# Latent attention rebuilt with keys on the partitions: the sums of probabilities added up in SBUF by GpSimd, one product with ones per batch

## The reference

```python
def layernorm(x, g, b):
    mu = jnp.mean(x, axis=-1, keepdims=True)
    var = jnp.mean(jnp.square(x - mu), axis=-1, keepdims=True)
    return (x - mu) * jax.lax.rsqrt(var + LN_EPS) * g + b

def rmsnorm(x, gamma):
    n = jnp.linalg.norm(x, axis=-1, keepdims=True) * x.shape[-1] ** (-0.5)
    return x / jnp.maximum(n, RMS_EPS) * gamma
xn = layernorm(x, ln_x_g, ln_x_b)            # x here: the context
ln = layernorm(latents, ln_l_g, ln_l_b)      # latents: the tokens
q = ln @ W_q
kv = jnp.concatenate([xn @ W_kv, ln @ W_kv], axis=1)
...
qn = rmsnorm(q, q_gamma) * SCALE
kn = rmsnorm(k, k_gamma)
sim = jnp.einsum('bhid,bhjd->bhij', qn, kn)
sim = jnp.where(full_mask[:, None, None, :], sim, neg)
attn = jax.nn.softmax(sim.astype(jnp.float32), axis=-1).astype(sim.dtype)
out = jnp.einsum('bhij,bhjd->bhid', attn, v)
...
return out @ W_out + b_out
```

## Time and profile before

| | us |
|---|---|
| median of 3 runs (6344.28 to 6349.45) | 6347.48 |
| the profiled execution | 6344.81 |
| its span, first to last instruction | 6343.0 |
| TensorE busy over the span (mean granted clock 0.840) | 4691.1 |
| latent sublayer, first transfer issued to last instruction | 3683.22 to 4145.88 |

### The profile page before, as it was taken

How to read it: one execution, slowest core, us unless ns; L and a number is a source line. 1 busy time by engine, 2 the same in 40 slices (tenths; PEclk the granted TensorE clock), 3 DMA queues, 4 the chain that set the end, 5 groups by cost and what they waited for, 6 DMA issues and landing times. The chain is left out here.

```text
span 6343.0 us, 136570 instructions
## 1 busy us (share of the span) xinstructions
PE 4691.1 (74%) x46654; PEld 2666.1 (42%) x46654; DVE 3568.5 (56%) x6692; ACT 2632.4 (42%) x5390; POOL 1186.4 (19%) x2741
## 2 busy tenths in 40 slices
PE   1101766785757989595888557789999999999997
PEld 0101222332332222243333245566676667666674
DVE  7897433544436666434333533266776677676775
ACT  0101632452635756251111111156665666656664
POOL 0000100010100101110000000034444344443442
PEclk6555878896968989696999755589999999999998
DMA  1000000000000000000000000010000000000000
GB/s 28 0 0 2 1 10 14 1 1 3 1 31 1 1 1 1 11 1 20 24 22 23 8 4 0 0 41 6 9 20 9 20 6 24 5 24 5 13 16 10
DMA packets 46808, 66.67 MB, mean 11 GB/s; under 512 B 8628, under 2 KB 40480, under 8 KB 44977
## 3 DMA queue, kind: packets, MB, share of 16 engines
q1 hardware_dynamic: 45564, 58.16, 3.1%
q0 software_dynamic: 784, 1.80, 0.1%
HBM read 53.22 MB, written 1.05 MB: 9 GB/s over the span
## 5 line engine op out<-in xcount | busy, mean ns | idle before, releaser
L647 DVE TENSOR_REDUCE minus_max<-banks 128x1 f32<-128x512 f32 (+4 forms) x1152 | 608.4, 570 | 308.7 <-PE banks L541 300.5
L611 ACT ACTIVATE probs<-banks 128x512 f32<-128x512 f32 (+4 forms) x1152 | 580.7, 554 | 349.3 <-PE banks L579 344.2
L2345 POOL TENSOR_TENSOR loc_cos_part<-loc_cos_part,loc_sin_part 128x512 f32<-128x512 f32 x388 | 494.1, 1274 | 741.5 <-DVE loc_sin_part L2774 741.3
L592 PE MATMUL banks<-probs,pair_rows 128*32 128x512 f32 (+3 forms) x2304 | 564.8, 573 | 0.2 <-ACT probs L611 0.2
L2418 PE MATMUL banks<-loc_w_qkv,loc_shifted 128*128 (+1 forms) x1552 | 416.1, 414 | 81.8 <-issue 66.5
L1301 DVE TENSOR_TENSOR product<-gated,banks 128x512 f32<-128x512 f32 x168 | 115.6, 688 | 489.9 <-ACT gated L1283 489.9
L1842 PE MATMUL banks<-identity,srt_c 128*128 128x128 f32 x64 | 13.6, 370 | 492.8 <-DVE srt_c L1970 492.8
L212 POOL TENSOR_SCALAR fin_shifted<-fin_moments 128x4 f32<-128x4 f32 x48 | 14.4, 299 | 1901.2 <-DVE fin_moments L298 1901.2
L1283 ACT ACTIVATE gated<-banks 128x512 f32<-128x512 f32 x168 | 100.3, 597 | 612.6 <-PE banks L1239 612.6
L2418 PEld LDWEIGHTS banks<-loc_w_qkv,loc_shifted 128*128 128x128 f32 x1552 | 295.8, 201 | 128.9 <-issue 68.8
L2771 DVE TENSOR_TENSOR loc_cos_part<-banks,loc_table 128x512 f32<-128x512 f32 x388 | 264.5, 682 | 73.8 <-ACT loc_square L2639 73.6
(11 more groups left out here) (471 smaller groups left out, 10180.4 us busy)
## 6 DMA issues: line engine op xcount, KB each, us to landing
expert_w<-in_L_ffn_pairs_dram SPq DMA_DIRECT2D x84, 192.0 KB, 2.4
loc_w_qkv<-in_L_ffn_Wqkv_dram SPq DMA_DIRECT2D x7, 1536.0 KB
q_stack<-max_rows SPq DMA_DIRECT2D x384, 3.0 KB
loc_v_edge<-loc_v SPq DMA_DIRECT2D x192, 32.0 KB, 1.8
fixed_w<-in_L_ffn_experts_dram SPq DMA_DIRECT2D x8, 514.5 KB, 4.1
loc_pack<-in_L_ffn_pack_dram SPq DMA_DIRECT2D x6, 537.5 KB, 4.3
loc_w_o<-in_L_ffn_Wo_dram SPq DMA_DIRECT2D x6, 512.0 KB, 4.1
loc_scales<-in_L_ffn_scales_dram SPq DMA_DIRECT2D x7, 256.0 KB, 8.0
```

Of the source, the lines that this page charges most:

```text
L592: ins = nc.tensor.matmul(o_bank[at:at + COLS, q0:S], pair_rows[u][:, k, e, :], probs[(a * C + k) % RING][e][:, q0:S], start=(k == 0), stop ...
L611: nc.scalar.activation(probs[(a * C + k) % RING][e][0:kn, q0:S], t_bank[e][0:kn, q0:S], ACT.Exp, scale=scale).then_inc(s["exp_done"], 1)
L647: nc.vector.tensor_reduce(minus_max[:, u, e, qs[0]:qs[0] + len(qs)], view, AX.X, ALU.max, negate=True).then_inc(s["max_done"], 1)
L2345: nc.gpsimd.tensor_tensor(cos_part[:, tiles, :], cos_part[:, tiles, :], sin_part[:, tiles, :], ALU.add).then_inc(s["summed"], 1)
```

## The change

The sublayer becomes three steps that share tiles: `latent_projections` (q, k, v for all four batches), `latent_heads` (attention for all), and `finish(..., "turned", ...)`, where the heads already stand with features on the partitions, so that the transposes and their copies fall away. The block that only loaded weights is gone; SyncE issues the transfers in the first block, beside the first statistics.

In `latent_projections` the batches are unrolled. TensorE's order is turn(0), and for each batch products(b), turn(b+1), means(b). The products now put features on the partitions (512 columns at a time), the squares are ScalarE's, their mean over a head is a product with a matrix of 1/64 (`means`), and the inverse root is ScalarE's Ln and then Exp with scale -0.5, three and two instructions per batch. VectorE's order per batch is copy_k(b), statistics(b+2), normalise(b+1), scale(b).

In `latent_heads` the scores are computed twice: `direct`, with queries on the partitions, only for the maxima (as before, but both heads at a time), and `turned`, with keys on the partitions, for exp. The maximum is split in three bf16 parts by GpSimd, turned by TensorE (`turn_maxima`), and added to the turned scores by a product with ones. So the probabilities come out with keys on the partitions, and neither transposes nor copies stand ahead of the product with v. The sum over keys: GpSimd adds the six key tiles of a head together in SBUF (`add`), and one product with ones per head and batch (`sums`) adds over the partitions. Head e uses rows 64e to 64e+63 of TensorE in `direct` and `turned`, and its columns in `values` and `sums`. RING = 4 buffers of probabilities per head, two pairs of `totals`.

```diff
@@ finish @@
+    if source == "turned":
+        pe.wait_ge(s["y_copied"], b + 1)
+        for t in range(QT):
+            ins = nc.tensor.matmul(g.bank[2 + u][:, t * P:(t + 1) * P],
+                                   y_now[:, u, t * P:(t + 1) * P], w_out[:, :],
+                                   start=True, stop=False)
+            ins = nc.tensor.matmul(g.bank[2 + u][:, t * P:(t + 1) * P],
+                                   g.ones[0:1, 0:P], bias_row[0:1, :],
+                                   start=False, stop=True)
...
@@ latent_projections, tensor @@
+def products(b):
+    u = b % 2
...
+    nc.tensor.matmul(g.bank[2][:, :], w_q[:, :], zT[u][:, 0:S], start=True, stop=True)
+    nc.tensor.matmul(g.bank[3][:, :], w_kv[:, 0:D], zT[u][:, 0:S], start=True,
+                     stop=True).then_inc(s["products_ready"], 1)
+    for t in range(QT, TILES):
+        nc.tensor.matmul(g.bank[4][:, (t - 2) * P:(t - 1) * P], zT[u][:, t * P:(t + 1) * P],
+                         w_kv[:, D:2 * D], start=True, stop=True)
+    nc.tensor.matmul(g.bank[4][:, 0:2 * P], w_kv[:, 0:D], zT[u][:, S:ALL], start=True,
+                     stop=True).then_inc(s["products_ready"], 1)
...
+def means(b):
+    pe.wait_ge(s["squared"], b * 3 + 3)
+    pe.wait_ge(s["q_copied"], b + 1)
+    if b:
+        pe.wait_ge(s["log_done"], b * 3)
+    lhs = mean_of[:, :, :].rearrange("p h d -> p (h d)")
+    for bank, c0, c1 in ((g.bank[2][:, 0:2 * P], 2 * S, S + ALL), (g.bank[6][:, :], 0, S),
+                         (g.bank[7][:, :], S, 2 * S)):
+        nc.tensor.matmul(bank, lhs, square[:, c0:c1], start=True, stop=True).then_inc(s["mean_ready"], 1)
...
+turn(0)
+for b in range(B):
+    products(b)
+    if b + 1 < B:
+        turn(b + 1)
+    if b == 0:
+        pe.wait_ge(s["setup"], 4)
+    means(b)
@@ latent_projections, scalar and vector @@
+def inverses(b):
+    for i, (bank, c0, c1) in enumerate(((g.bank[2][:, 0:2 * P], 2 * S, S + ALL), (g.bank[6][:, :], 0, S),
+                                        (g.bank[7][:, :], S, 2 * S))):
+        act.wait_ge(s["mean_ready"], b * 3 + i + 1)
+        nc.scalar.activation(log[:, c0:c1], bank, ACT.Ln).then_inc(s["log_done"], 1)
+    if b:
+        act.wait_ge(s["scaled"], b * 2)
+    act.wait_ge(s["log_done"], b * 3 + 3)
+    for c0, c1 in ((0, S), (S, S + ALL)):
+        nc.scalar.activation(inverse[:, c0:c1], log[:, c0:c1], ACT.Exp, scale=-0.5).then_inc(s["inverse_done"], 1)
+copy_zT(0)
+for b in range(B):
+    squares(b)
+    if b + 1 < B:
+        copy_zT(b + 1)
+    inverses(b)
...
+for b in range(B):
+    copy_k(b)
+    if b + 2 < B:
+        statistics(b + 2)
+    if b + 1 < B:
+        normalise(b + 1)
+    scale(b)
@@ latent_heads @@
+def direct(b, q):
+    n = b * QT + q
+    if n:
+        pe.wait_ge(s["max_done"], n * 2)
+    here = slice(q * P, (q + 1) * P)
+    for e in range(HEADS):
+        nc.tensor.matmul(g.bank[2 + e][:, 0:CTX], ones_bf[half(e), :], bias_rows[half(e), b, :],
+                         start=True, stop=False, skip_group_check=True)
+    for e in range(HEADS):
+        nc.tensor.matmul(g.bank[2 + e][:, 0:CTX], qT[b][half(e), here], kT[b][half(e), S:S + CTX],
+                         start=False, stop=True, skip_group_check=True)
+    for e in range(HEADS):
+        nc.tensor.matmul(g.bank[e][:, :], qT[b][half(e), here], kT[b][half(e), 0:S],
+                         start=True, stop=True).then_inc(s["direct_ready"], 1)
+def turn_maxima(b):
+    pe.wait_ge(s["third_done"], b + 1)
+    if b:
+        pe.wait_ge(s["rows_copied"], b)
+    for q in range(QT):
+        ins = nc.tensor.matmul(x_bank[:, q * P:(q + 1) * P],
+                               max_parts[:, q, :, :].rearrange("p e i -> p (e i)"), g.ident_bf[:, :],
+                               start=True, stop=True)
+    ins.then_inc(s["max_turned"], 1)
+def turned(b, k):
+    m = b * TILES + k
+    if k == 0:
+        pe.wait_ge(s["rows_copied"], b + 1)
+    if m:
+        pe.wait_ge(s["exp_done"], m * 2)
+    for e in range(HEADS):
+        nc.tensor.matmul(g.bank[4 + e][:, :], ones_bf[half(e), :], max_rows[half(e), :],
+                         start=True, stop=False, skip_group_check=True)
+    for e in range(HEADS):
+        nc.tensor.matmul(g.bank[4 + e][:, :], kT[b][half(e), k * P:(k + 1) * P], qT[b][half(e), :],
+                         start=False, stop=True, skip_group_check=True).then_inc(s["turned_ready"], 1)
+def values(b, k):
+    m = b * TILES + k
+    pe.wait_ge(s["exp_done"], m * 2 + 2)
+    if k == 0 and b:
+        pe.wait_ge(s["heads_done"], b)
+    for e in range(HEADS):
+        ins = nc.tensor.matmul(o_bank[half(e), :], v[b][:, k, half(e)], buffer(b, k, e)[:, :],
+                               start=(k == 0), stop=(k == LAST), skip_group_check=True)
+        if e:
+            ins.then_inc(s["values_done"], 1)
+def sums(b):
+    pe.wait_ge(s["added"], (b + 1) * LAST * HEADS)
+    if b:
+        pe.wait_ge(s["sum_log_done"], b)
+    for e in range(HEADS):
+        ins = nc.tensor.matmul(sum_bank[half(e), :], ones[:, :], totals[b % 2][e][:, :],
+                               start=True, stop=True, skip_group_check=True)
+    ins.then_inc(s["sums_ready"], 1)
...
+for q in range(QT):
+    direct(0, q)
+turn_maxima(0)
+for b in range(B):
+    for k in range(TILES):
+        turned(b, k)
+        if b + 1 < B and k < QT:
+            direct(b + 1, k)
+        if b + 1 < B and k == LAST:
+            turn_maxima(b + 1)
+        if k:
+            values(b, k - 1)
+        elif b:
+            values(b - 1, LAST)
+            sums(b - 1)
+values(B - 1, LAST)
+sums(B - 1)
+def exps(b, k):
+    m = b * TILES + k
+    kn = narrow if k == LAST else P
+    bias = g.zero[0:kn, 0:1] if k < QT else bias_columns[0:kn, b, k - QT:k - QT + 1]
+    j = b * LAST + k - RING
+    old_b, old_k = (b - 1, LAST) if k == LAST else (j // LAST, j % LAST)
+    if old_b >= 0:
+        act.wait_ge(s["values_done"], old_b * TILES + old_k + 1)
+        act.wait_ge(s["added"], (old_b * LAST + (old_k or 1)) * HEADS)
+    for e in range(HEADS):
+        act.wait_ge(s["turned_ready"], m * 2 + e + 1)
+        nc.scalar.activation(buffer(b, k, e)[0:kn, :], g.bank[4 + e][0:kn, :], ACT.Exp,
+                             bias=bias).then_inc(s["exp_done"], 1)
...
+def inverse_sums(b):
+    act.wait_ge(s["sums_ready"], b + 1)
+    if b:
+        act.wait_ge(s["heads_done"], b)
+    nc.scalar.activation(sum_log[:, :], sum_bank[:, :], ACT.Ln).then_inc(s["sum_log_done"], 1)
+    act.wait_ge(s["sum_log_done"], b + 1)
+    nc.scalar.activation(sum_inv[:, :], sum_log[:, :], ACT.Exp, scale=-1.0).then_inc(s["sum_inv_done"], 1)
...
+copy_rows(0)
+for b in range(B):
+    for k in range(TILES):
+        exps(b, k)
+        if k == 0 and b:
+            inverse_sums(b - 1)
+        if k == LAST and b + 1 < B:
+            copy_rows(b + 1)
+inverse_sums(B - 1)
+def add(b, k):
+    pool.wait_ge(s["exp_done"], (b * TILES + k) * 2 + 2)
+    if k == 1 and b >= 2:
+        pool.wait_ge(s["sums_ready"], b - 1)
+    for e in range(HEADS):
+        total = totals[b % 2][e]
+        if k > 1:
+            pool.wait_ge(s["added"], (b * LAST + k - 2) * HEADS + e + 1)
+        first = buffer(b, 0, e) if k == 1 else total
+        nc.gpsimd.tensor_tensor(total[:, :], first[:, :], buffer(b, k, e)[:, :],
+                                ALU.add).then_inc(s["added"], 1)
...
+split(0)
+for b in range(B):
+    for k in range(1, TILES):
+        if k == LAST and b + 1 < B:
+            split(b + 1)
+        add(b, k)
...
+    nc.vector.tensor_reduce(maxima[:, u, :, q, 0], g.banks[:, 0:2, :], AX.X, ALU.max).then_inc(s["max_done"], 1)
+    nc.vector.tensor_reduce(maxima[:, u, :, q, 1], ctx_scores, AX.X, ALU.max).then_inc(s["max_done"], 1)
...
+def heads(b):
+    dve.wait_ge(s["sum_inv_done"], b + 1)
+    dve.wait_ge(s["values_done"], (b + 1) * TILES)
+    nc.vector.tensor_tensor(headsT[:, b * S:(b + 1) * S], o_bank[:, :], sum_inv[:, :],
+                            ALU.mult).then_inc(s["heads_done"], 1)
```

More of the change, by code:

```diff
@@ L2007, in latent_attention_3 @@
[L2007 to L2013, removed]
@@ new lines, in source, with statistics @@
+                def source(b, t):
+                    return g.x[:, b * QT + t, :] if t < QT else context[:, b, t - QT, :]
+                def statistics(b):
+                    u = b % 2
+                    if b == 0:
+                        for t in range(TILES):
+                            if t == QT:
+                                dve.wait_ge(s["loaded"], 96)
+                            nc.vector.bn_stats(stats[:, u, t, :], source(b, t)).then_inc(s["stats_done"], 1)
+                    else:
+                        for t in range(TILES):
+                            nc.vector.bn_stats(stats[:, u, t, :], source(b, t)).then_inc(s["stats_done"], 1)
+                    dve.wait_ge(s["stats_done"], (b + 1) * TILES)
+                    if b >= 2:
+                        dve.wait_ge(s["shift_done"], b - 1)
```

(32 more changed lines are left out.)

360 lines of the change are left out of this document (195 added, 165 removed).

## The result

| | kernel before | changed kernel |
|---|---|---|
| median of 4 runs each, same chip | 6346.25 us (6344.28 to 6349.45) | 6048.53 us (6044.80 to 6049.84) |
| ratio, 95% interval | | 0.953 (0.951 to 0.955) |
| span of the profiled execution | 6343.0 us | 6047.7 us |
| latent sublayer | 462.7 us | 235.6 us |
| local attention behind it, whose code is the same | 2195.6 us | 2126.2 us |

Forecast: 6140, range 6116 to 6192. Of the 295.3 us that the span lost, the latent sublayer gave 227.1 (207.9 forecast) and the local attention, of which the forecast says nothing, 69.4. The other 1.2 us went the other way, ahead of the sublayer. So of the 91.5, the local attention makes 69.4 and the sublayer 19.2; the rest is those 1.2 and the distance of the two medians from their profiled executions.

What follows compares the result with a forecast made beforehand. Sublayer bound by TensorE at the low clock plus serial waits. Terms 13.4 + 61.4 + 4.5 + 18.4 + 4 + 111.4 + 41.7 = 254.8 against 462.7 us, 207.9 less: 6136.9, with the median's 2.7 6140, range 6116 to 6192.

Steps and rivals of the forecast that it cites:

- sublayers never overlap: it is enough to price one: Whole kernel: only the latent sublayer, 462.7 us, was priced, with no term for any other sublayer.
- start to first products: Start of the sublayer: products begin about 13.4 us after the first transfer issue, against 16.6 before, a gain of 3.
- projections: Four batches of q, k, v: cycles of 17, 16 and 14 us and 14.4 for the last, 61.4 us.
- into the heads: Between projections and heads: block end and semaphore clearing 2.9 us, memsets 1.6, together 4.5.
- directs, split, turn, copy: Before the first batch of heads: four directs in series 18.4 us, then split, turn_maxima and copy_rows 4.
- four batches: Heads: first batch 26 us, two inner ones 28.2 each, last 29, sum 111.4.
- finish, with the clearing: End of the sublayer: 2.9 us of clearing plus 38.8 for finish, without turning and copying out the heads: 41.7.
- slot 5: Key tile k = 5 in the heads: turn_maxima waits for the split queued behind GpSimd's adds, slot becomes 6.2 us.
- rival A: Heads: float32 pairs of 64 rows run one after the other, +58 us, 6198; chance 0.12.
- Rival B: Heads: the clock stays low, slots 0 to 3 at 7.0 us, total 6185; chance 0.12.
- Rival C: ScalarE's Ln and Exp in the sublayer: no table reloads, -15.4 us, 6125; chance 0.13.
- Rival D: Heads: GpSimd's 40 serial adds become the bound from 8.0 us per add; at 9 us, 6388; chance 0.02.

Runs made afterwards that it cites:

- experiment 5: 128 idle semaphore increments on TensorE's queue, placed where it waits for transfers: kernel before 6345.0 to 6282.7 us, changed kernel 6052.7 to 6123.4.
- experiment 3: Two separate edits of the changed kernel: one table set for Ln and Exp loaded once, 6038.3 us; split one add pair earlier, 6043.6 us.

## Why the prediction was wrong

**The step that failed** is in the first paragraph: "sublayers never overlap: it is enough to price one". They don't overlap, but they share TensorE's instruction stream, and the place of a later loop in it is moved by every instruction added or removed ahead. The row was there: [3.04 <-issue] in the earlier trace rows, with eight instructions in 3.68 us behind it, was used to price a clock drop and not asked what it was. With the local attention at its old 2195.6 us the median would have been 6048.5 + 69.4 = 6118, just inside the range. No case of the forecast had a term outside the sublayer; the 69.4 are an accident of place, and could as well have been a loss: between the two padded kernels of experiment 5 the same edit moves the loop from a cheap place to an expensive one, and the local attention goes from 2131.9 to 2200.7 us.

**The terms of the sum** were 19 us too high (254.8 against 235.6):

| step | forecast | measured |
|---|---|---|
| start to first products | 13.4 | 12.5 |
| projections | 61.4 | 56.2 |
| into the heads | 4.5 | 4.1 |
| directs, split, turn, copy | 22.4 | 20.2 |
| four batches | 26 + 28.2 + 28.2 + 29 = 111.4 | 23.8 + 25.9 + 25.1 + 27.1 = 101.9 |
| finish, with the clearing | 41.7 | 40.6 |

- *Projections*: 5.2 of the error. The first products of one batch and the next are 15.8, 14.1 and 13.0 us apart and the last batch takes 13.2, where I had 17, 16, 14 and 14.4. The loads were not dearer than thought by much: without them (experiment 3) the way from the first transfer to the first turned product is 86.4 us instead of 93.1, five loads' worth where four were priced. So it is the cycles without loads that were priced too high, all four of them.
- *Batches*: 9.5. The slot with direct was right (3.42 for 3.4), the slot without too (2.69 for 2.85), slot 5 too (6.05 for 6.2), though partly by luck: its products with v ran at the lower clock, which I had priced outside the slot, and that made up for a split priced too high. The pair of turned products took 0.86 to 0.95 side by side, so rival A, worth +58, is out. What I priced too high: the split, four steps of 0.22 us with 1.1 in all where I had 2.3 from L2361's 0.49, and the wait for the heads, 1.04 instead of 2.6 in the inner batches.
- *Rival B* (clock low in the heads): not so; 0.89 from the first turned product on and 1.00 in the full slots. With the directs (0.50) the stretch is at 0.82, below the 0.85 that I had named as a sign.
- *Rival C and the table loads*: 16 loads of 1.283 us, as assumed; taking them away gave 15.9 us where 15.4 were priced. The Trainium skill (ScalarE: Activation LUTs, "Table sets: the hidden batching unit") has a single load for ln and then exp; in these runs that holds only once the set is asked for, and unasked, Ln and Exp reload each time. The drain of 1.38 us that the Trainium skill (the same page, "What ACT_TABLE_LOAD costs") adds to every switch is not there: the engine idles 0.1 us ahead of four loads.
- *Rival D* (GpSimd bound at 8.0 us an add): 1.27 measured. GpSimd mattered through the order of split and adds, 10.7 us, which was priced as part of slot 5 and confirmed by moving it, and through the last pair of adds, for which TensorE waits 1.49 us ahead of the last sums.

What stays open: how a place in the stream turns into idle time. The map of the kernel before has five points; the length of 256 instructions that I had assumed is refuted, and no other was measured; that it follows the 16 KB packets is suggested by their count, not shown.

## What to carry to other kernels

Before pricing an edit, look for loops behind it and for idle time marked "issue" at their first instruction: that cost depends on where the loop lies in its engine's stream, and an edit anywhere ahead moves it. When an unchanged part gets faster or slower, pad the stream by instructions that cost nothing and see whether the difference moves with them, before crediting the edit. And a side engine that is far from full can still hold the critical one by the order of its queue; put the short step that others wait for ahead of the long ones.

## What the runs showed of the hardware

- The same loop of TensorE, with the same work, cost 1.4 to 3.4 us of idle time at each jump back, by its place in the stream alone, and with the lower clock behind the longer idle 62 to 71 us over 22 jumps.
- An increment of a semaphore on TensorE's queue takes 0.15 us, by the differences: 18.0, 27.7, 37.5 and 45.9 us of idle for 64, 128, 192 and 246 of them.
- Pairs of float32 products of 64 rows, on the two halves of the rows, run side by side: 0.86 to 0.95 us for two of 512 columns at the high clock.
- GpSimd adds of 128x512 float32 take 1.27 us beside TensorE, ScalarE and VectorE at work on the same tiles, as long as in the local attention.
